# A decoder layer with routed experts: the experts in two batches, the first batch's tiles woven into the eighth group

## The reference

```python
# layer, cut: names as in the kernel
x1   = x + green(potentials(layernorm(x)))          # tridiagonal resolvent, by continued fractions
xheb = x1 + hebbian(layernorm(x1)) @ w_out          # 8 heads, decayed fast weights
x2   = x + xheb + gelu_tanh(layernorm(xheb) @ w_ff1) @ w_ff2
xa   = layernorm(x2)
xb   = layernorm(xa + cross_attention(xa, ctx))     # 16 heads of 8
top2, gate = route(xb @ Wr.T)                       # 2 of 8 experts, softmax over the two
out  = layernorm(xb + sum_k gate_k * (gelu(xb @ W1[e_k] + b1) @ W2[e_k] + b2))
```

## Time and profile before

| | us |
|---|---|
| median of 3 runs | 757.51 |
| lowest, highest | 754.78, 759.88 |
| span of the profiled execution | 767.7 |
| TensorE busy, of that span | 663.8 |
| DVE busy | 504.3 |
| ScalarE busy | 400.6 |
| POOL busy | 321.2 |

### The profile page before, as it was taken

The page is one execution under the profiler, slowest core; times in us unless marked ns, Lnnn a source line. Parts: engine busy times, 40 slices in busy tenths (PEclk is TensorE's granted clock), DMA queues, the critical chain, the costliest instruction groups (busy, mean ns, idle before and its releaser), DMA issues.

```text
span 767.7 us, 20050 instructions
## 1 busy us (share of the span) xinstructions
PE 663.8 (86%) x6278; PEld 493.5 (64%) x6278; DVE 504.3 (66%) x1733; ACT 400.6 (52%) x855; POOL 321.2 (42%) x463
## 2 busy tenths in 40 slices
PE   9779898898998998998998989888888999999920
PEld 9664756755755764764774765674443999999920
DVE  4586568768679669668678777773624555555535
ACT  0212365484475375475465466544320677767716
POOL 6104362354364264265166157136014355444535
PEclk8579999999999999999999999999989999999965
DMA  8600000000000000000000000000032322222144
GB/s 294 214 1 14 2 29 17 1 25 14 4 25 14 4 21 14 7 21 11 11 18 14 11 0 32 11 0 29 1 111 86 78 72 72 71 68 73 53 173 173
DMA packets 26058, 36.23 MB, mean 47 GB/s; under 512 B 7302, under 2 KB 18311, under 8 KB 25736
## 3 DMA queue, kind: packets, MB, share of 16 engines
q1 hardware_dynamic: 20582, 22.72, 9.6%
q0 software_dynamic: 4576, 9.53, 3.6%
q10 hardware_dynamic: 850, 3.38, 1.3%
HBM read 23.99 MB, written 12.63 MB: 48 GB/s over the span
## 4 chain that ended last, share of the span: by engine, by line
PE 53%; DVE 15%; issue 12%; POOL 9%; ACT 6%; DMA 3%; SPq 1%; ACTq 1%; DVEq 1%; POOLq 0%
PE bank L1893 8%; PE bank L1903 8%; PE bank L1561 8%; PE bank L1735 4%; ACT mix L555 4%; POOL rstd L737 3%; PE bank L1597 3%; PE bank L1721 3%; PE bank L1701 3%; PE bank L1646 2%; PE bank L1654 2%; PE bank L1547 2%; POOL vare L734 2%; PE bank L1484 2%; POOL expert_in L779 1%
## 5 line engine op out<-in xcount | busy, mean ns | idle before, releaser
L779 POOL DMA_INDIRECT expert_in<-xb_rows,slot_u x72 | 73.2, 1016 | 103.5 <-PE bank L1711 49.0
L871 POOL DMA_INDIRECT expert_out<-xa,v_sb x71 | 68.3, 962 | 77.5 <-issue 47.3
L675 ACT ACTIVATE hT<-bank,qT 128x128 f32<-128x128 f32 x284 | 80.9, 368 | 36.6 <-issue 19.4
L734 POOL TENSOR_SCALAR vare<-mv 128x1 f32<-128x1 f32 (+1 forms) x108 | 23.8, 220 | 166.4 <-DVE mv L1064 166.1
L1186 DVE TENSOR_REDUCE negmax<-bank 128x4 f32<-128x512 f32 x128 | 79.4, 683 | 7.9 <-PE bank L1701 7.9
L555 ACT ACTIVATE mix<-bank 128x512 f32<-128x512 f32 x128 | 66.1, 605 | 24.9 <-PE bank L1721 24.9
L1903 PE MATMUL bank<-w_t,hT 128*128 x568 | 75.4, 276 | 1.1 <-ACT hT L675 1.1
L1893 PE MATMUL bank<-xnT,qT 128*128 128x128 f32 x568 | 75.1, 276 | 1.1 <-DVE qT L1400 1.1
L737 POOL TENSOR_TENSOR rstd<-vare,minus_half 128x1 f32<-128x1 f32 (+1 forms) x108 | 66.5, 616 | 9.6 <-POOL vare L734 1.2
L1903 PEld LDWEIGHTS bank<-w_t,hT 128*128 128x128 f32 x568 | 69.1, 192 | 1.8 <-issue 1.7
L1893 PEld LDWEIGHTS bank<-xnT,qT 128*128 128x128 f32 x568 | 69.0, 192 | 1.4 <-DVE qT L1400 1.4
(11 more groups left out here) (300 smaller groups left out, 1483.6 us busy)
## 6 DMA issues: line engine op xcount, KB each, us to landing
...
x_all<-expert_out SPq DMA_DIRECT2D x4, 512.0 KB, 10.5
...
```

What stands on the lines that cost most here:

```text
L675: ins = nc.scalar.activation(hx[j % 2][:, c, :], bank[2 + j % 2][:, c * P:(c + 1) * P], ACT.Gelu, bias=w1c[j % 2][:, FF + c:FF + c + 1])
L779: nc.gpsimd.indirect_dma_start(xs[:, :], bass.IndirectOffsetOnAxis(ap=slot_u[:, t, k:k + 1], axis=0), xb_rows[k][:, t, :], None).then_inc( ...
L871: nc.gpsimd.indirect_dma_start(ys[:, :], bass.IndirectOffsetOnAxis(ap=tag[j % ROWS][:, HOME - P:HOME - P + 1].bitcast(U32), axis=0), ysb[j ...
```

## The change

- The experts work in two batches. Batch 0 is the first six groups (24 sequences, 48 + 7 = 55 tiles, `TA`), batch 1 the last two (16 + 7 = 23 tiles): 78 tiles in all. Each has its own `expert_in`, `expert_out` and table. DVE computes batch 0's table in three pieces inside the seventh group (`tile_counts`, `tile_starts`, `tile_table`), batch 1's between tiles 26 and 28. SP alone writes the pads.
- The eighth group has no spins. On every engine its steps alternate with tiles 0 to 25 in a new hand-written order; `LAST_JOBS` and `BANK_LAST` give the group four of the banks (7, 2, 5, 4), the tiles use 1, 0, 6 and 3. Up to tile 30 there is one output bank: `outputs(j)` waits until the results of j - 1 are drained. From tile 31 there are two.
- Rows are turned two tiles at a time (`turn_pair`) and copied by DVE as one 128x256 copy (`feed`, which has the w1 copy too). `FEED` = 3 buffers of w1 and hx, 15 of rows, 8 of results.
- Gates are doubled (`wsum` = 0.5 + 0.5 ratio), so that both copies add the row itself: the sum of the two is twice the value, which the last norm takes out (4 EPS). `own_rows` is gone.
- `gelu_table` (one activation of one element) loads the Gelu table on ScalarE after each `exps` and after the ratios.
- The results of groups 0 to 5 are read back after tile 54 and added (now on POOL, `halves_added`), scaled, shifted, normed and stored between tiles 61 and 77. Groups 6 and 7 follow after the last tile.
- w2 (2 MB) is loaded over `x_all` during the seventh group.

```diff
-TILES = SEQS * TOPK + EXP - 1
-UNROLL = 4
-ROWS = 12
+BATCH_GROUPS = (6, 2)
+BATCH_SEQS = tuple(n * T for n in BATCH_GROUPS)
+BATCH_TILES = tuple(n * TOPK + EXP - 1 for n in BATCH_SEQS)
+REGIONS = tuple((n + EXP) * P for n in BATCH_SEQS)
+TILES = sum(BATCH_TILES)
+TA = BATCH_TILES[0]
+AG = BATCH_GROUPS[0]
+YBUFS = 8
+ROWS = 15
+FEED = 3
 RW = P + 4
-HOME, GATE, OWN = P, P + 1, P + 2
-PADS = EXP + TILES - SEQS * TOPK
-REGION = (SEQS + TILES - SEQS * TOPK + 1) * P
+HOME, GATE = P, P + 1
+B_PADS_AT = 42
+PADS = 2 * EXP - 1
...
+BANK_LAST = dict(zip(LAST_JOBS, map(int, "725472547254725472" + 4 * "72547725472" + "54725472")))
...
+ROW_BANK, HIDDEN_BANKS = 1, (0, 6)
+ONE_OUT, OUT_BANKS = 31, (3, 4)
...
+            filled(sp, AG, f"ks{XC - 1}")
+            load_context(AG * GT + GT)
+            sp.wait_ge(ends_ready, 1)
+            pad(sp, 0)
+            sp.wait_ge(scattered, 16 * (AG + 1) * T * TOPK)
             sp.sem_inc(xb_free, 1)
...
+            sp.wait_ge(xf_ready, G)
+            sp.wait_ge(xbk_ready, G + 1)
+            sp.dma_start(w2_t, A["w2_t"]).then_inc(w2_loaded, 16)
+            sp.wait_ge(table_ready, 1)
...
+            filled(sp, AG, "hpv3")
+            sp.wait_ge(padded, 16 * EXP)
+            for j in range(B_PADS_AT):
+                row_in(j)
+            sp.wait_ge(ends_ready, 2)
+            pad(sp, 1)
+            for j in range(B_PADS_AT, TA):
+                row_in(j)
+            sp.wait_ge(table_ready, 2)
+            sp.wait_ge(padded, 16 * 2 * EXP)
+            sp.wait_ge(scattered, 16 * (SEQS + T) * TOPK)
+            for j in range(TA, TA + ROWS):
+                row_in(j)
+            for n in range(YBUFS):
+                sp.wait_ge(y_out[n], 16 * len(range(n, TA, YBUFS)))
+            filled(sp, G - 1, "xpv3")
...
+            for g in range(AG):
+                rows_back(0, g)
+            for j in range(TA + ROWS, TILES):
+                row_in(j)
+            def result_out(g):
                 sp.wait_ge(outc_ready, g + 1)
                 sp.sem_inc(sp_held, 1)
+                sp.dma_start(A["out"][:, g * T:g * T + T, :], acc[g][:, :, :]).then_inc(stored[g % 2], 16)
+            for g in range(AG):
+                result_out(g)
+            for n in range(YBUFS):
+                sp.wait_ge(y_out[n], 16 * len(range(n, TILES, YBUFS)))
+            for g in range(AG, G):
+                rows_back(1, g)
...
+            g = G - 1
+            first_layer(g)
+            for c in range(XC):
+                placed_keys(g, c)
+            gelu(0)
+            gelu(1)
+            drain(g, "xaT", xnT[:, :])
+            gelu(2)
+            queries_high(g)
+            gelu(3)
+            placed_queries(g, 0)
+            placed_queries(g, 2)
+            gelu(4)
+            for t in range(T):
+                o = 4 + 4 * t
+                gelu(o + 1)
+                gelu(o + 2)
+                exps(g, t)
+                gelu_table()
+                attended(g, t)
+                gelu(o + 3)
+                gelu(o + 4)
+            drain(g, "cxT", cxT[:, :])
+            gelu(21)
+            gelu(22)
+            gelu(23)
+            drain(g, "xbT", xnT[:, :])
+            second_rows(g)
+            gelu(24)
+            gelu(25)
+            gelu(26)
+            ratios(g)
+            gelu_table()
+            for j in range(27, TA + 10):
                 gelu(j)
...
+            for j in range(TA + 10, TILES):
+                gelu(j)
+                if (j - TA) % 2 == 0 and (j - TA - 10) // 2 < AG:
+                    last_norm((j - TA - 10) // 2)
...
+            g = G - 1
+            row_out(1, 0, 0)
+            row_out(1, 0, 1)
+            row_out(1, 1, 0)
+            row_out(1, 1, 1)
+            for t in range(T):
+                ln_scale(LNA, g, t)
+            row_out(1, 2, 0)
+            row_out(1, 2, 1)
+            results_out(0)
+            row_out(1, 3, 0)
+            results_out(1)
+            row_out(1, 3, 1)
+            output_bias(g)
+            for j in range(2, 20):
                 results_out(j)
+            for t in range(T):
+                ln_scale(LNB, g, t)
+            for j in range(20, 25):
+                results_out(j)
+            rows_chosen(g)
+            for j in range(25, 33):
+                row_out(1, (j - 25) // TOPK, (j - 25) % TOPK)
+                results_out(j)
...
+            for j in range(33, TILES):
+                if (j - TA) % 2 == 0 and 0 <= (j - TA - 6) // 2 < AG:
+                    halves_added((j - TA - 6) // 2)
+                results_out(j)
+                if (j - TA) % 2 == 0 and 0 <= (j - TA - 8) // 2 < AG:
+                    last_scale((j - TA - 8) // 2)
...
+                if g is AG:
+                    tile_counts(0)
...
+                if g is AG:
+                    tile_starts(0)
+                maxima(g, 0)
...
+                if g is AG:
+                    tile_table(0)
+                decayed(g, 0)
...
+            def feed(j):
+                if j >= FEED:
+                    dve.wait_ge(gelu_done, j - FEED + 1)
+                ins = nc.vector.tensor_copy(w1c[j % FEED], w1_t[:, bass.ds(experts[j], 1), :].rearrange("p a n -> p (a n)"))
+                if j % 2 == 0:
+                    dve.wait_ge(turned, j // 2 + 1)
+                    ins = nc.vector.tensor_copy(xqT[:, j % 4 * P:(j % 4 + 2) * P], bank[ROW_BANK][:, 0:2 * P])
+                ins.then_inc(fed, 1)
...
+            def results_of(j):
+                if j > 0:
+                    weighed(j - 1)
+                results(j)
+                if j + 4 < TILES:
+                    if j + 4 == TA:
+                        dve.wait_ge(table_ready, 2)
+                    experts.append(expert_of(j + 4))
...
+            feed(0)
+            feed(1)
+            feed(2)
+            dve.wait_ge(xsum_ready, G)
+            for t in range(T):
+                after_ff(g, t)
+            for t in range(T):
+                ln_apply(LNA, g, t, x2[:, t, :], xa[:, t, :])
+            results_of(0)
+            feed(3)
+            results_of(1)
+            queries_low(g)
+            feed(4)
+            results_of(2)
+            placed_queries(g, 1)
+            placed_queries(g, 3)
+            feed(5)
+            results_of(3)
+            feed(6)
+            for t in range(T):
+                o = 4 + 4 * t
+                maxima(g, t)
+                results_of(o)
+                shifted(g, t)
+                feed(o + 3)
+                results_of(o + 1)
+                feed(o + 4)
+                results_of(o + 2)
+                feed(o + 5)
+                normalise(g, t)
+                results_of(o + 3)
+                feed(o + 6)
+            results_of(20)
+            feed(23)
+            dve.wait_ge(xab_ready, G)
+            for t in range(T):
+                output_step(g, t)
+            results_of(21)
+            output_step(g, T)
+            output_step(g, T + 1)
+            feed(24)
+            dve.wait_ge(scattered, 16 * SEQS * TOPK)
+            homes(g)
+            for t in range(T):
+                ln_apply(LNB, g, t, x2[:, t, :], xb[:, t, :])
+            results_of(22)
+            feed(25)
+            results_of(23)
+            feed(26)
+            best_experts(g)
+            choices(g)
+            results_of(24)
+            feed(27)
+            results_of(25)
+            gates(g)
+            slots(g)
+            nc.vector.tensor_copy(slot_u[:, :, :], slot_f[:, :, :]).then_inc(slot_ready, 1)
+            drained(dve, g, "rank")
+            feed(28)
+            results_of(26)
+            tile_counts(1)
+            feed(29)
+            results_of(27)
+            tile_starts(1)
+            feed(30)
+            results_of(28)
+            tile_table(1)
...
+            for j in range(29, TILES):
+                if j + 2 < TILES:
+                    feed(j + 2)
+                if (j - TA) % 2 == 0 and 0 <= (j - TA - 10) // 2 < AG:
+                    shift((j - TA - 10) // 2)
+                results_of(j)
+                if (j - TA) % 2 == 0 and 0 <= (j - TA - 8) // 2 < AG:
+                    moments((j - TA - 8) // 2)
...
+                if j == ONE_OUT:
+                    b = OUT_BANKS[1]
+                    pe.wait_ge(free[b], (G - 1) * PER_GROUP[b] + FIRST[b] + LAST[b] + 1)
+                elif j > 0:
+                    pe.wait_ge(y_drained, j if j < ONE_OUT else j - 1)
+                pe.wait_ge(gelu_done, j + 1)
...
+            turn_pair(0)
             hidden(0)
...
+            place_keys(g)
+            hidden(1)
+            second_layer(g)
+            pe.wait_ge(table_ready, 1)
+            pe.wait_ge(w2_loaded, 16)
+            outputs(0)
+            hidden(2)
+            turn(g, "xaT", LNA, g, xa)
+            outputs(1)
+            all_queries(g)
+            hidden(3)
+            outputs(2)
+            place_queries(g)
+            hidden(4)
+            outputs(3)
+            for t in range(T):
```

(34 more changed lines are left out.)

1016 lines of the change are left out of this document (460 added, 556 removed), and 6 rows, old and new, of the table LAST_JOBS.

## The result

| | before | changed |
|---|---|---|
| median of the runs, us | 758.0 (4 runs) | 776.1 (4 runs) |
| range, us | 754.8 to 759.9 | 771.6 to 778.1 |
| ratio, 95% interval | | 1.0245 (1.0203 to 1.0287) |
| span of the profiled execution, us | 767.7 | 774.4 |

The change makes the kernel 2.5% slower; 737 was predicted, 2.7% faster, with a range of 720 to 757. The profiled execution of before spans 9.7 us more than its median, so a second one was taken (first experiment). After's span of 774.4 agrees with its median.

The account below looks back on a forecast made before the run. Tiles bound by TensorE, the eighth group by its chain of steps, the end by engine hand-overs. 515.9 + 2.5 + 106.6 + 2.0 + 88.4 + 10 + 2.0 + 19.7 = 747.1; less the profile's 10.2 excess: 737 us, range 720 to 757.

Parts of the forecast that it names:

- The seventh group: First batch's table on DVE in the seventh group, partly covered by idle: adds 2.5 us, range 0 to 4.5.
- The early outputs: Tiles 61 to 73, finishing the first six groups' outputs alongside: adds 10 us, range 0 to 15.
- shift waits for the scale: Early outputs: DVE's shift waits for POOL's scale, feeds stand behind it, so TensorE gets POOL's pace, 5.5 per two tiles.
- POOL never idle: Sign to look for: 5.5 to 5.8 us per two tiles while the early adds run, POOL always working.
- The pace of all tiles: Tiles on TensorE: 1.90 us each, so 88.4 for the 47 O and 46 H after the eighth group.
- The first layer to O(30): Eighth group woven with tiles: 24.1 first part, 52.0 four sequences, 30.5 end, 106.6 us; clock 2.0 more.
- The walk: One sequence of the eighth group followed step by step: 13.0 us, 2.5 of it waiting, set by ScalarE's order.
- the idle ahead of the first H: Eighth group's start: TensorE waits 3.3 us while DVE loads four experts.
- The tail: From the last O to the end: 19.7 us where it was 33.65, six groups being normed and stored earlier.
- Rival 4: TensorE held at 1.2 GHz through the whole woven eighth-group stage: +63.8, 801 us; chance 0.08.
- Rival 3: Hand-overs dearer: 15.5 a sequence (+10) or 15 for POOL's pace (+5), 742 to 752 us; chance 0.12.
- Rival 2: Table switches hold ScalarE longer than the 1.28 load, 8 us over the four sequences: 745 us; chance 0.08.

Follow-up runs that it names:

- first experiment: The kernel before, unedited, profiled a second time: 757.9 us, span 756.0.
- 8: On top of 7, the seventh group's table work split into places where VectorE waited, the last piece at the group's end: 742.9 us (0.9801).
- 9: As 8, with the table's last piece moved earlier, behind the first sum of the associative memory's output: 734.3 us (0.9686).
- 2: Changed kernel with the seventh group's six one-number additions moved behind the last shifted scores, just ahead of the table: 771.5 us (1.0164).
- 5: Changed kernel with the early shift and early normalising of the first six groups one pair of tiles later: 763.6 us (1.0083).
- 12: Changed kernel with the edits of 5, 7 and 9 together, outputs still early: 740.3 us (0.9772).
- 14: As 12, without VectorE's loads of the expert from tile 62 on (expert 0 taken, wrong weights): 736.1 us.
- 7: On top of 3, VectorE's load of the expert of tile j + 4 put ahead of the sum of tile j: 751.7 us (0.9909).
- experiment 10: On top of 9, three of the six late additions of halves on VectorE instead of GpSimd: 731.4 us (0.9654).
- 6: Changed kernel with Gelu in place of the eighth group's exponentials, so no table loads within the four sequences: 778.6 us.
- 3: Changed kernel with the first six groups' outputs finished behind the last tile, rows still read back early: 756.6 us (1.0001).

## Why the prediction was wrong

**The seventh group, 2.5 predicted, 13.1 measured: the step that failed.** Its cost was taken as VectorE's time less the idle beside it, 0 to 4.5. The durations were right (1.1 for the additions where nothing holds them, 3.4 for the table). Missing were the neighbours: GpSimd's additions at that moment, one of which the earlier trace rows show with 1.29, held VectorE for 3; and TensorE's clock, which I had only put to the new stage, fell behind the stalls, 7.6 of the 14.0. The same work in VectorE's waits cost 0 to 0.4 (8, 9), and the group fell from 55.0 to 40.2 by it. Moving the additions alone gave 6.6 of it in the traces, 4.5 in the medians (2). "SBUF — State Buffer" of the Trainium skill, section "SBUF: two separate sides", says that VectorE and GpSimd share a pair of ports as an exclusive lock, which concerns VectorE's operations with two inputs in SBUF, beside one of GpSimd that reads SBUF, and its copies in a mode that takes two ports. The 3.09 us addition and the copy of 1.45 beside a 1.28 addition agree with it; the addition was held over a scatter's issue and both of GpSimd's additions, not over one instruction alone.

**The early outputs, +10 predicted (0 to 15), +25 measured: the step that failed.** GpSimd's pace of 5.5 per two tiles was right as GpSimd's sum: with slack the runs show 6.0 per pair on average (5), and 5.4 with the load ahead of the sum (12), where the steady step is 5.5. What failed is "shift waits for the scale", which I had read as giving TensorE GpSimd's pace. In truth the wait closed a ring over four engines inside one pair of tiles, 7.8 long, in which GpSimd was idle for 19.3 of 46 us, and its stalls brought the clock to 0.84. "POOL never idle" was the observation I had named, and it is the one that fell. Slack won 8.8 of the 25 in these tiles, and no early step 23.7. What sets the pace that is left is only in part known (14).

**The pace of all tiles, 1.90 predicted, 2.02 measured.** I had counted no cost for VectorE's load of the expert behind the sum instead of ahead of it. That is 6.1 us on 47 tiles (7). The code of before has the load ahead of the sum; the two orders should have been compared.

**The first layer to O(30), 108.6 with the clock, 115.1 measured: near, with two terms too small.** In experiment 10, with the load first and the clock at 1.00, it is 23.7, 14.5, 12.8, 12.8 and 42.4 for the last sequence and the end, 106.2 in sum against my 106.6. The 8.9 between that and 115.1 are the clock, 4.3 of them in the first part and the first sequence against 2.0 predicted for the whole, and the place of the load, which I had at nothing. Part of the agreement is luck. The walk gave the 13.0 to ScalarE's order with its `gelu_table`; without any load of a table the sequence took as long (6), since VectorE's order gives about the same time. And the idle ahead of the first H was 2.1, not 3.3. (Two slips of the sum are small: the waits listed for the end of the group add up to 6.35, not 6.5, and three loads in 2.56 are 0.85 each, not 0.82.)

**The tail, 19.7 predicted, 18.2 measured: right.** Six groups out of it save 15. Done early, though, they cost more than that.

**The base.** The difference of the profile to the median (10.2) was carried over as if it were the same in both. 5.7 of the 11.7 us between before's two profiles lie in stages that the change replaces, so with the second profile as the base my own sum would have given 14.9 saved, not 20.6, and a forecast of 743.

**The rivals.** Slower was the outcome, but by none of the named ways. Rival 4 (clock) had the right kind of mechanism mostly in the wrong place: the new stage reads 0.80 to 1.00, the seventh group and the early outputs 0.84 each, with 7.6 and 7.9 us of it. Rival 3 had the right one, dearer hand-overs at GpSimd, priced at +5 where it was +15. Rival 2 fell: the exponentials end at 574.73, the load at 574.75 takes 1.28 and the activation follows at 576.05, against the drain that "ScalarE: Activation LUTs" of the Trainium skill states in "What ACT_TABLE_LOAD costs". With the table and the load in their places and without early outputs the weaving does what was forecast of it, and more: 734.3, and 731.4 with the additions shared.

The loss from 758 to 776 in sum: the weaving and the shorter tail gain, and the seventh group (13), the ring (25 for 9 of tail) and the load's place (6) take it back. In the medians, each of which carries the up to 4 us of the clock in the eighth group's start, the steps of experiments 3, 7, 8 and 9 gave 19.5, 4.9, 8.8 and 8.6.
